# One-hot slot tables in 16 bits, with the 32 token-and-expert columns innermost

## The reference, cut to what matters

```python
xn = _layernorm(x, axis=-1)
x = x + _L0_attn_ref(xn, ...) + _L0_ffn_ref(xn, ...)
...
probs = jax.nn.softmax(x @ router_w.T, axis=-1)
w = _top_p_weights(probs, TOP_P)         # 0 where the expert is not taken
for e in range(n_exp):
    g = jax.nn.silu(x @ gate_w[e].T)
    u = x @ up_w[e].T
    y = g * u @ down_w[e].T
    out = out + y * w[:, e:e + 1]
```

## Time and profile before

| what | value |
|---|---|
| median of three runs | 926.46 us |
| the three runs | 923.11, 926.46, 931.77 us |
| the profiled execution's own time | 922.48 us |
| its span, first to last instruction | 920.8 us |
| mean granted TensorE clock | 0.945 |
| PE busy | 789.1 us (86%) |
| DVE busy | 573.1 us (62%) |
| ACT busy | 347.0 us (38%) |
| POOL busy | 402.2 us (44%) |
| DVE busy of 44.50 us in one steady block, 183.50 to 228.00 us | 35.28 us |
| PE busy in the same block | 39.73 us |

### The profile page before, as it was taken

How to read it: one execution, slowest core, us unless ns; L and a number is a source line. 1 busy time by engine, 2 the same in 40 slices (tenths; PEclk the granted TensorE clock), 3 DMA queues, 4 the chain that set the end, 5 groups by cost and what they waited for, 6 DMA issues and landing times.

```text
span 920.8 us, 21143 instructions
## 1 busy us (share of the span) xinstructions
PE 789.1 (86%) x7104; PEld 718.4 (78%) x7105; DVE 573.1 (62%) x1262; ACT 347.0 (38%) x770; POOL 402.2 (44%) x397
## 2 busy tenths in 40 slices
PE   5889898898989897388898887988987989889993
PEld 5767677676767676388898887988987979888993
DVE  5788787878786957645556465455555565565442
ACT  3133333333424252344344443343443443443441
POOL 3010101010101015546667577576657566676663
PEclk9899999999999997689999999999999999999997
DMA  3111120202020204212524335324325324333332
GB/s 116 70 47 51 42 87 5 92 0 92 0 92 0 70 2 150 52 36 44 123 47 80 93 47 121 51 46 126 53 40 120 52 46 115 52 52 58 58 58 35
DMA packets 38419, 57.99 MB, mean 63 GB/s; under 512 B 4096, under 2 KB 33792, under 8 KB 37376
## 3 DMA queue, kind: packets, MB, share of 16 engines
q0 software_dynamic: 19776, 27.16, 18.4%
q1 hardware_dynamic: 18624, 30.59, 9.6%
HBM read 35.58 MB, written 22.15 MB: 63 GB/s over the span
## 4 chain that ended last, share of the span: by engine, by line
PE 33%; DVE 24%; issue 16%; DMA 10%; ACT 9%; POOL 4%; ACTq 2%; POOLq 1%; DVEq 1%
DMA out<-ybuf,s_idx 7%; PE A L1040 6%; PE A L1042 6%; PE A L1041 6%; DVE h L1021 4%; DVE s_sb L764 4%; PE S L1078 3%; ACT h_hi L692 3%; DVE h_lo L1023 3%; DMA xg<-gather_table,g_idx 3%; PE O L1040 2%; PE O L1042 2%; PE O L1041 2%; PE O L1105 1%; ACT sg L690 1%
## 5 line engine op out<-in xcount | busy, mean ns | idle before, releaser
L373 POOL DMA_INDIRECT out<-ybuf,s_idx x104 | 173.8, 1671 | 59.7 <-POOL s_idx L461 42.7
L1040 PE MATMUL A<-gT_hi,w_hi 128*128 128x256 f32 x588 | 168.4, 286 | 4.7 <-issue 3.2
L1023 DVE TENSOR_TENSOR h_lo<-h,h_hi 128x256 fp32r<-128x256 f32 x196 | 110.0, 561 | 94.8 <-ACT h_hi L692 94.8
L1041 PE MATMUL A<-gT_lo,w_hi 128*128 128x256 f32 x588 | 167.1, 284 | 0.0
L1042 PE MATMUL A<-gT_hi,w_lo 128*128 128x256 f32 x588 | 166.9, 284 | 0.0
L1040 PE MATMUL O<-w_hi,h_hi 128*128 128x256 f32 x392 | 119.5, 305 | 19.1 <-DVE h_lo L1023 19.1
L356 POOL TENSOR_TENSOR kf<-kz 128x256 f32<-128x256 f32 x16 | 18.9, 1184 | 257.8 <-DVE kz L759 257.8
L448 POOL DMA_INDIRECT xg<-gather_table,g_idx x100 | 100.6, 1006 | 62.1 <-POOL g_idx L446 43.2
L692 ACT ACTIVATE h_hi<-h 128x256 fp32r<-128x256 f32 x196 | 81.9, 418 | 109.5 <-DVE h L1021 109.5
L1040 PEld LDWEIGHTS A<-gT_hi,w_hi 128*128 128x128 f32 x588 | 113.8, 194 | 6.6 <-issue 6.5
L1041 PEld LDWEIGHTS A<-gT_lo,w_hi 128*128 128x128 f32 x588 | 113.5, 193 | 0.0
(11 more groups left out here) (181 smaller groups left out, 1641.0 us busy)
## 6 DMA issues: line engine op xcount, KB each, us to landing
w_raw<-wffn SPq DMA_DIRECT2D x8, 1536.0 KB, 6.5
gather_table<-xna SPq DMA_DIRECT2D x8, 528.0 KB
xa<-x SPq DMA_DIRECT2D x8, 512.0 KB, 3.5
xr<-x SPq DMA_DIRECT2D x8, 512.0 KB, 4.8
out<-yout SPq DMA_DIRECT2D x8, 512.0 KB
out<-ybuf,s_idx POOLq DMA_INDIRECT x104, 3.9
xg<-gather_table,g_idx POOLq DMA_INDIRECT x100
w_raw<-wqk_nat SPq DMA_DIRECT2D x1, 512.0 KB, 5.2
```

The costliest lines, as they stand in the source:

```text
L373: pool.indirect_dma_start(out=out, out_offset=bass.IndirectOffsetOnAxis(ap=s_idx[:, sub:sub + 1], axis=0), in_=ybuf[:, sub, :], in_offset= ...
L1023: v.tensor_tensor(h_lo[:, ic, :], h[:, ic, :], h_hi[:, ic, :].bitcast(F32), ALU.subtract).then_inc(hlo_ok, 1)
L1040: mm(out_ap, l_hi, r_hi, start=(k == 0), stop=False)
L1041: mm(out_ap, l_hi, r_lo, start=False, stop=False)
```

## The change

The three tables get a new order of dimensions and the inputs of the comparisons become 16-bit. Before, a table was (column, number) with the numbers innermost; now it is (number, column), with the 32 columns innermost. `lo_iota` and `hi_iota` are written out over the 32 columns, as BF16; `slot_lo` and `slot_hi` are BF16. `one_hot` now handles half of the 128 numbers for all 32 columns in one call, so there are two calls of 2048 elements in place of four of 1024. The call in front of `queries` goes away; the two calls in front of `head_norm` are one. The products of `slot_tokens` read their weight and their moving operand with a step of 32 elements (64 bytes).

```diff
-        lo_iota = sb("lo_iota", [P, P])
-        hi_iota = sb("hi_iota", [P, NT // P])
+        lo_iota = sb("lo_iota", [P, P, TT * NE], BF16)
+        hi_iota = sb("hi_iota", [P, NT // P, TT * NE], BF16)
...
-        slot_lo = sb1("slot_lo", [P, TT, NE])
-        slot_hi = sb1("slot_hi", [P, TT, NE])
-        oh_lo = sb1("oh_lo", [P, TT * NE, P], BF16)
-        oh_hi = sb1("oh_hi", [P, TT * NE, NT // P])
-        oh_rhs = sb1("oh_rhs", [P, TT * NE, 2, NT // P], BF16)
+        slot_lo = sb1("slot_lo", [P, TT * NE], BF16)
+        slot_hi = sb1("slot_hi", [P, TT * NE], BF16)
+        oh_lo = sb1("oh_lo", [P, P, TT * NE], BF16)
+        oh_hi = sb1("oh_hi", [P, NT // P, TT * NE], BF16)
+        oh_rhs = sb1("oh_rhs", [P, 2, NT // P, TT * NE], BF16)
...
-            g.iota(lo_iota[:, :], pattern=[[1, P]], base=0, channel_multiplier=0, allow_small_or_imprecise_dtypes=True)
-            g.iota(hi_iota[:, :], pattern=[[P, NT // P]], base=0, channel_multiplier=0,
+            g.iota(lo_iota[:, :, :], pattern=[[1, P], [0, TT * NE]], base=0, channel_multiplier=0,
+                   allow_small_or_imprecise_dtypes=True)
+            g.iota(hi_iota[:, :, :], pattern=[[P, NT // P], [0, TT * NE]], base=0, channel_multiplier=0,
...
-                a.activation(oh_rhs[:, :, 0, :], oh_hi[:, :, :], ACT.Copy, scale=part[:, 0:1])
+                a.activation(oh_rhs[:, 0, :, :], oh_hi[:, :, :], ACT.Copy, scale=part[:, 0:1])
                 for t in range(TT):
                     e = slice(t * NE, (t + 1) * NE)
-                    last = a.activation(oh_rhs[:, e, 1, :], oh_hi[:, e, :], ACT.Copy, scale=tile_no[:, t:t + 1])
+                    last = a.activation(oh_rhs[:, 1, :, e], oh_hi[:, :, e], ACT.Copy, scale=tile_no[:, t:t + 1])
...
-                v.tensor_tensor(oh_hi[:, :, :], hi_iota[:, :].unsqueeze(1).to_broadcast([P, n, NT // P]),
-                                hi.unsqueeze(2).to_broadcast([P, n, NT // P]), ALU.is_equal).then_inc(slot_ok, 1)
+                v.tensor_tensor(oh_hi[:, :, :], hi_iota[:, :, :], slot_hi[:, :].unsqueeze(1).to_broadcast([P, NT // P, n]),
+                                ALU.is_equal).then_inc(slot_ok, 1)
...
-            def one_hot(s, t):
-
-                ins = v.tensor_tensor(oh_lo[:, t * NE:(t + 1) * NE, :], lo_iota[:, :].unsqueeze(1).to_broadcast([P, NE, P]),
-                                      slot_lo[:, t, :].unsqueeze(2).to_broadcast([P, NE, P]), ALU.is_equal)
-                if t == TT - 1:
+            def one_hot(s, part):
+
+                lo = slice(part * P // 2, (part + 1) * P // 2)
+                ins = v.tensor_tensor(oh_lo[:, lo, :], lo_iota[:, lo, :],
+                                      slot_lo[:, :].unsqueeze(1).to_broadcast([P, P // 2, TT * NE]), ALU.is_equal)
+                if part == 1:
                     ins.then_inc(lo_ok, 1)
...
-                    one_hot(s - 1, 2)
-                    one_hot(s - 1, 3)
+                    one_hot(s - 1, 1)
                     head_norm(s - 1, 1, chain)
...
-                one_hot(s, 1)
                 if not last:
                     queries(s + 1, 0)
...
-                        o = mm(idx_bank[:, e * 64:(e + 1) * 64], oh_lo[:, n, :],
-                               oh_rhs[:, n, :, :].rearrange("p a n -> p (a n)"), start=(t == 0), stop=(t == TT - 1))
+                        o = mm(idx_bank[:, e * 64:(e + 1) * 64], oh_lo[:, :, n],
+                               oh_rhs[:, :, :, n].rearrange("p a h -> p (a h)"), start=(t == 0), stop=(t == TT - 1))
```

More of the change, by code:

```diff
@@ L816, in slots @@
                 chain.link(v.tensor_scalar(lo_i[:, :, :], slot_i[:, :, :], P - 1, None, ALU.bitwise_and))
-                chain.link(v.tensor_copy(slot_lo[:, :, :], lo_i[:, :, :]))
-                chain.link(v.tensor_tensor(slot_hi[:, :, :], slot[:, :, :], slot_lo[:, :, :], ALU.subtract))
+                flat = lambda a: a[:, :, :].rearrange("p t e -> p (t e)")
                 n = TT * NE
-                hi = slot_hi[:, :, :].rearrange("p t e -> p (t e)")
-                v.tensor_tensor(oh_hi[:, :, :], hi_iota[:, :].unsqueeze(1).to_broadcast([P, n, NT // P]),
-                                hi.unsqueeze(2).to_broadcast([P, n, NT // P]), ALU.is_equal).then_inc(slot_ok, 1)
+                chain.link(v.tensor_copy(slot_lo[:, :], flat(lo_i)))
+                chain.link(v.tensor_tensor(slot_hi[:, :], flat(slot), slot_lo[:, :], ALU.subtract))
+                v.tensor_tensor(oh_hi[:, :, :], hi_iota[:, :, :], slot_hi[:, :].unsqueeze(1).to_broadcast([P, NT // P, n]),
+                                ALU.is_equal).then_inc(slot_ok, 1)
                 v.tensor_scalar(from_end[:, :], from_end[:, :], float(-BLK), None, ALU.add)
                 chain.link(v.tensor_copy(base[:, 0, :], base[:, TT, :]))
-            def one_hot(s, t):
-                ins = v.tensor_tensor(oh_lo[:, t * NE:(t + 1) * NE, :], lo_iota[:, :].unsqueeze(1).to_broadcast([P, NE, P]),
-                                      slot_lo[:, t, :].unsqueeze(2).to_broadcast([P, NE, P]), ALU.is_equal)
-                if t == TT - 1:
+            def one_hot(s, part):
[3 more added lines that the diff above has]
+                if part == 1:
                     ins.then_inc(lo_ok, 1)
@@ L973, in _ @@
             second_half(NBLK - 1, True, chain)
-            one_hot(NBLK - 1, 2)
-            one_hot(NBLK - 1, 3)
+            one_hot(NBLK - 1, 1)
             add_indices(NBLK - 1)
```

## The result

| | before | after |
|---|---|---|
| median of four runs each, us | 925.91 (923.11 to 931.77) | 942.70 (936.72 to 946.01) |
| profiled execution's own time, us | 922.48 | 946.01 |
| its span, us | 920.8 | 944.3 |
| mean granted clock | 0.945 | 0.923 |
| PE busy, us | 789.1 | 829.9 |

The changed kernel is slower: 1.0127 times the time before, with a 95% interval of 1.0071 to 1.0184 (the two medians are further apart, 16.8 us or 1.8%, at the upper end of that interval). I had forecast 918 us and a range of 908 to 940. The comparisons did get faster, and PE got slower: in the first phase DVE is busy 17 us less (296.8 and 279.4 us) and PE 31 us more (328.9 and 360.4). The whole execution shows 8 less and 41 more, because both engines were busy 9 us longer in the experts' phase, whose code is the same.

The account below looks back on a forecast made before the run. The prediction took the first phase's chain of waits, alternating between PE and DVE, as the bound. DVE -8.3, products +2.4 and clock -2.9 sum to -8.8 us; from the median 926.46 that gives 917.7, forecast 918 us, range 908 to 940.

Parts of the forecast that it names:

- The comparisons on DVE: 16-bit `oh_lo` and `oh_hi` run at twice the rate, saving 0.77 + 0.54 = 1.3 us per pair of halves, -8.3 us in all.
- The wait for the keys: PE's 0.58 us idle time before `kz` in a steady block, forecast to vanish as DVE and ACT run earlier.
- I take 65 ns, nearer to the lower end: Price of one load and matmul pair in `slot_tokens` with the 64-byte step: 2.1 us a block, 1.0 more than before.
- rival 2: Products in `slot_tokens` at about 115 ns a pair, 3.7 us a block, eat the gain: about 0, 927 us; chance 0.25.
- The surplus d: Extra time of a block's 32 products in `slot_tokens` over the kernel before, forecast at 1.0 us and hidden in steady blocks.
- the cover of 1.7 us: Time in a steady block between the end of `slot_tokens` and DVE reaching `add_indices`, forecast to hide longer products.
- The clock: Falls of the granted clock to 0.50 behind PE's gap before `scores(s, 7)`: two of five guessed to go, -2.9 us.
- the six pairs: `second_half(s)` with `first_half(s + 1)`, s = 0 to 5, in the first phase: forecast 1.3 us saved each, 7.8 us together.
- Setup: hidden, with 2 us to spare: POOL's longer iotas at the start take at most 9.6 us and end before `t2k` needs the last memset: no cost.
- The two open places, +2.4: Last block and end of the first phase, where longer products are never hidden: 1.2 us each.
- ACT, "nothing": ACT's activations keep their element counts; four writing in runs of 8 elements were forecast to cost nothing extra.
- Rival 3: Dear products make DVE wait in `add_indices`, outweighing its gain from 3.0 us extra; at 175 ns a pair +19, 945 us; chance 0.20.

## Why the prediction was wrong

Three terms of the sum failed: the price of a product with the 64-byte step, which was put too low; the clock, which was booked as a gain; and the setup, which was put at nothing. The gain on DVE was right, and the dear products took most of it back. The steps, as the prediction puts them:

- **The comparisons on DVE, "a rate twice as high", 1.3 us for each pair of halves: right.** `oh_lo` takes 1.22 us for 2048 elements, `oh_hi` 0.69 (forecast: near 0.66). What this is worth shows only where the products are cheap. With a step of 2 the blocks are 41.8 us without a fall, 43.0 before, and 43.4 with one, 44.5 before: 1.1 to 1.2 us for the forecast 1.3. The wait for the keys is gone and the one before `scores(s, 7)` is 1.19 us, forecast 1.2.
- **"I take 65 ns, nearer to the lower end": mis-sized.** That was the step of the sum that failed first. 3.73 us for 32 pairs are 117 ns, rival 2's 115. The surplus d is 2.6 us and not 1.0, beyond the cover of 1.7 us, and `add_indices` comes late by 0.88 us, as rival 2 has it (0.9). This takes most of DVE's gain of 1.3 us in each of the steady blocks. The path was right (cover, then DVE in `add_indices`); the size was not. The value had been chosen by likeness to the products' own row, which said nothing of steps; the bounds, 35 and 291 ns, were right and the value sat too near the lower one.
- **The clock, "two of five is my guess, -2.9 us": wrong, in sign too.** No fall went; there is one in every steady block, twice as long. With the right d the six pairs should come to -2.4 us (rival 2). Measured are +4.1 and -0.7, so there remain +6.5 us in one pair of profiles and +1.7 in the other for the clock and whatever else is not in the sum. The larger is against an execution in which the kernel before had no fall in two of its blocks, the smaller against one where it had them all. So a longer fall seems to cost little more than a short one here, 0.3 us a block; as I read it, part of it is taken from the gap of 1.2 us that PE would have had anyway (after, there is none before 237.53). What costs is a fall where there had been none: 44.5 us a block for 43.0. Two falls were booked as gone with no run or row behind the number; the prediction called it a guess, and it was one.
- **"Setup: hidden, with 2 us to spare": wrong, +3.6 us.** The reader of the last memset wasn't held up. I had asked only who reads what POOL makes, and not which DVE instructions run while POOL does. `var_eps` (1.18 us before, 2.53 after) and `xna` (1.38, 3.21) were held up. The kernel with the iotas alone shows 2.6 of the 3.6 us, the one with late iotas takes away 3.4. The iotas themselves were cheaper than the bound: 4.18 and 1.13 us, for the 9.6 put for both.
- **The two open places, +2.4: mis-sized.** The products there cost 1.8 us more each (3.50 for 1.71 and 3.57 for 1.75), for the 1.2 that I took: 3.6 in all. In the last pair this is made up, since from `scores(6, 7)` to the products it is 1.8 us shorter in both pairs of profiles (39.2 for 41.0, and 39.3 for 41.1), for a forecast of 0.5. How much of that is DVE's is open: before, the fall at 318.5 us lies behind `scores(6, 7)`, after, the one at 318.4 us in front of it. Behind `scores(7, 7)` nothing makes it up: +2.1 and +3.2 us, of which 0.3 and 1.4 stand in front of the products. The chain of waits of the kernel after, the two products and what stands between:

```profile
365.56 3.50 PE A L1119 x32
...
384.92 1.49 POOL on_lo L362
...
389.38 3.57 PE A L1119 x32
```

- **ACT, "nothing": right.** 1134 and 494 ns before, 1136 and 496 after; writes in runs of 8 elements are free, writes one by one are not (above).

With the right d, rival 2 gives 927 us from the median; without its -2.9 for the clock, and with 3.6 for the start, that is 933. By the ratio the change costs 0.0127 x 926 = 11.8 us, 6.6 to 17 by its interval, which is 938; the medians of four runs are 16.8 us apart. The first phases explain 10.9 us of it by one pair of profiles and 5.3 by the other. How much beyond that is the change's, through the clock or through the experts' phase, stays open: single profiles scatter by as much. Rival 3 had the right sign and the right wait, DVE in `add_indices`, but not by its own condition, d above 3.0; it needed the two terms outside the products, start and clock, to get there.

## What to carry to other kernels

A table should be packed for its reader on TensorE and its writer at once: groups of two columns innermost gave DVE its doubled rate and TensorE its full one, and that version beats both kernels (0.9889, 0.9836 to 0.9941), where 32 innermost lost 1.3%. Groups of four did as well in time (0.9871, 0.9824 to 0.9918), because this kernel hides 1.7 us of products in a block; how they would do with less cover was not run. Before a setup step is called hidden, look at what the neighbouring engine runs beside it, and not only at who reads its result. And a granted clock that varied between two executions of one kernel is a term with a range on both sides, not one from which a gain can be booked.

## What the runs showed of the hardware

- A 64-column bf16 matmul with its 128-column load takes 35 ns at a step of 2 bytes, 36 at 4, 68 at 8, 128 at 16 and 117 at 64. With the step in the weight alone (64 bytes) it is 66, in the moving operand alone 116.
- ACT took 5020 ns to write 1024 bf16 elements one by one, 64 elements apart, and 1134 in runs.
- An iota of 4096 bf16 values took 4.18 us on POOL, and a DVE `TENSOR_SCALAR` on 4 fp32 elements, begun during it, ended with it (2.53 us).
- In the steady blocks falls of the granted clock to 0.50 lasted 3.4, 6.8 or 10.2 us, and their number varied between two executions of one kernel (5 and 6 before, 3 and 2 with the step of 2). Side by side, 2.97 us of products left it at 1.00 in five of six blocks; products of 3.7 us in dear steps went with 6.8 us or more of 0.50 in every block. Why is open.
